# A one-core two-layer transformer kernel: eleven tile buffers, spaced row scatters and a later wait for counts in its tail

## What is computed

```
x = x + attn0(layernorm(x)) + ffn0(layernorm(x))
x = x + attn1(layernorm(x)) + moe(layernorm(x))
```

```
logits = xt @ Wg.T
topk_logits, topk_idx = top_k(logits, 2)
gates = zeros.at[rows, topk_idx].add(softmax(topk_logits))
h = gelu(einsum('th,ehi->tei', xt, W1) + b1)
y = einsum('te,teh->th', gates, einsum('tei,eih->teh', h, W2) + b2)
```

## Time and profile before

| what | value |
|---|---|
| median of 3 runs | 1271.79 us (1271.42 to 1272.31) |
| profiled execution, its own time | not listed |
| its span | 1269.4 us |
| mean granted TensorE clock | 0.982 |
| busy: PE, DVE, ACT, POOL | 1189.8, 848.0, 734.5, 665.2 us |
| chain that ended last | PE 63%, DVE 13%, ACT 10%, issue 6%, POOL 3%, DMA 3% |

### The profile page before, as it was taken

The page is one execution under the profiler, slowest core; times in us unless marked ns, Lnnn a source line. Parts: engine busy times, 40 slices in busy tenths (PEclk is TensorE's granted clock), DMA queues, the critical chain, the costliest instruction groups (busy, mean ns, idle before and its releaser), DMA issues.

```text
span 1269.4 us, 26751 instructions
## 1 busy us (share of the span) xinstructions
PE 1189.8 (94%) x9122; PEld 894.4 (70%) x9122; DVE 848.0 (67%) x3390; ACT 734.5 (58%) x1561; POOL 665.2 (52%) x921
## 2 busy tenths in 40 slices
PE   5988999999999999999999999999999857989996
PEld 2566777677767776777677767776776657885896
DVE  4066597659865986588658855886588646874563
ACT  2356367736773577357745774567456524557674
POOL 4574364536443644464446444644465436675677
PEclk9999999999999999999999999999999968999999
DMA  7704420432043304230423043304330056541333
GB/s 219 210 3 162 132 77 12 158 123 92 13 160 109 106 14 159 96 120 13 158 97 119 13 151 105 117 15 137 118 117 15 11 151 147 81 66 25 45 55 39
DMA packets 88039, 119.30 MB, mean 94 GB/s; under 512 B 13736, under 2 KB 46416, under 8 KB 85904
## 3 DMA queue, kind: packets, MB, share of 16 engines
q1 hardware_dynamic: 69312, 99.66, 25.2%
q0 software_dynamic: 13792, 9.54, 5.3%
q10 hardware_dynamic: 4800, 8.39, 2.0%
HBM read 70.78 MB, written 48.46 MB: 94 GB/s over the span
## 4 chain that ended last, share of the span: by engine, by line
PE 63%; DVE 13%; ACT 10%; issue 6%; POOL 3%; DMA 3%; SPq 0%; DVEq 0%; POOLq 0%; ACTq 0%
PE bank L708 18%; PE heads L766 13%; PE bank L701 12%; PE bank L680 7%; ACT probs L1119 5%; PE bank L676 3%; PE bank L691 2%; DVE xnT_s L1579 2%; POOL out L1361 2%; PE bank L1054 2%; DVE hrow L1579 2%; DVE hT_s L1579 2%; PE bank L816 2%; PE bank L1062 1%; PE bank L685 1%
## 5 line engine op out<-in xcount | busy, mean ns | idle before, releaser
L1119 ACT ACTIVATE probs<-bank 128x512 f32<-128x512 f32 (+2 forms) x896 | 443.3, 578 | 186.5 <-PE bank L708 180.2
L1308 POOL TENSOR_SCALAR_AFFINE_SELECT probs<-probs 128x384 f32<-128x384 f32 x256 | 127.4, 520 | 211.7 <-ACT probs L1119 211.2
L708 PE MATMUL bank<-K,Q 128*128 128x192 f32 (+4 forms) x1024 | 236.5, 308 | 0.0
L708 PE MATMUL bank<-Q,K 128*128 128x192 f32 (+4 forms) x1024 | 220.7, 322 | 3.3 <-ACT probs L1119 3.1
L766 PE MATMUL heads<-probs,V 128*18 128x192 f32 (+9 forms) x3072 | 196.1, 396 | 6.6 <-POOL probs L1311 3.9
L708 PEld LDWEIGHTS bank<-K,Q 128*128 128x128 f32 x1024 | 166.5, 189 | 21.7 <-issue 9.6
L708 PEld LDWEIGHTS bank<-Q,K 128*128 128x128 f32 x1024 | 152.3, 194 | 39.5 <-issue 17.5
L766 PEld LDWEIGHTS heads<-probs,V 128*9 128x9 f32 (+1 forms) x3072 | 78.5, 94 | 114.0 <-issue 75.6
L1361 POOL DMA_INDIRECT out<-h1T_s x78 | 123.1, 1578 | 60.0 <-ACT h1T_s L1269 35.6
L708 PE MATMUL bank<-QM,K 128*128 128x512 f32 (+3 forms) x512 | 138.4, 336 | 4.6 <-ACT probs L1119 3.8
L1261 ACT ACTIVATE h2T_s<-bank,h1T_s 128x128 f32<-128x128 f32 x312 | 89.2, 368 | 91.8 <-PE bank L1054 88.9
(11 more groups left out here) (224 smaller groups left out, 2184.9 us busy)
## 6 DMA issues: line engine op xcount, KB each, us to landing
Q<-slots_of_q SPq DMA_DIRECT2D x15, 1024.0 KB, 8.0
K<-low_of_h SPq DMA_DIRECT2D x13, 1024.0 KB, 7.8
QM<-slots_of_qm SPq DMA_DIRECT2D x8, 1024.0 KB, 6.0
K<-slots_of_k SPq DMA_DIRECT2D x60, 128.0 KB, 2.7
K<-slots_of_k SPq DMA_DIRECT2D x68, 96.0 KB
slots_of_q<-Q SPq DMA_DIRECT2D x24, 256.0 KB, 3.0
slots_of_k<-QM SPq DMA_DIRECT2D x24, 256.0 KB, 4.0
slots_of_qm<-Q SPq DMA_DIRECT2D x24, 256.0 KB, 4.2
```

The lines of the kernel that those rows point to most:

```text
L708: mm = pe.matmul(to[:, at:at + right.shape[1]], left, right, start=True, stop=True, skip_group_check=True)
L1119: return act.activation(to, bank, func, scale=scale, bias=bias).then_inc(taken_sem(run, unit), 1)
L1308: pool.affine_select(out=three, in_=three, compare_op=ALU.is_ge, fill=0.0, base=0, pattern=[[0, 3], [1, P]], channel_multiplier=-1)
```

## The change

- XB goes from 8 to 11. With it the early loads become tiles 0 to 10, then 11 and 12, the tail's loads start at tile 13, and run `lag` = 8 instead of 5 tiles ahead of `tiles_by(n)`, up to READY.
- `tile_xT` and `tile_b1` lie in w2T instead of behind the output buffers, since 11 * 130 + 4 * 128 leaves 106 values in `late`.
- SyncE waits for `pads_counted` behind the tail's first loads, ahead of the first pad, instead of ahead of everything in the tail.
- The eight scatters stand behind additions 16, 18, ... 30 instead of 16 to 23. The assertion holds with gated = 16.

```diff
-XB, OB, WB = 8, 4, 4
+XB, OB, WB = 11, 4, 4
...
-        tile_xT = late[:, XB * ROW + OB * P:XB * ROW + (OB + 2) * P].rearrange("p (n c) -> p n c", c=P)
-        tile_b1 = late[:, XB * ROW + (OB + 2) * P:XB * ROW + (OB + 2) * P + WB * FC].rearrange("p (n c) -> p n c", c=FC)
+        tile_xT = w2T[:, 0:2 * P].rearrange("p (n c) -> p n c", c=P)
+        tile_b1 = w2T[:, 2 * P:2 * P + WB * FC].rearrange("p (n c) -> p n c", c=FC)
...
                 run, lag = ("tail", NB), XB - 3
-                sp.wait_ge(S["pads_counted"], 1)
                 sp.wait_ge(S["routing_set"], ROUTING)
...
-                    if loaded < tiles_by(n) + lag:
-                        load_tiles(loaded, tiles_by(n) + lag)
-                        loaded = tiles_by(n) + lag
+                    if loaded < min(READY, tiles_by(n) + lag):
+                        load_tiles(loaded, min(READY, tiles_by(n) + lag))
+                        loaded = min(READY, tiles_by(n) + lag)
+                        if pads == 0:
+                            sp.wait_ge(S["pads_counted"], 1)
                         if pads < K2 * E:
...
             gated = tiles_by(9) + 1
+            assert gated + 2 * NT * K2 <= AT_MAXIMA + 1
             for i in range(QUERIED, AT_MAXIMA):
                 add_tile(i)
-                if gated <= i < gated + NT * K2:
-                    send_row((LAST, 0), i - gated)
+                if i in range(gated, gated + 2 * NT * K2, 2):
+                    send_row((LAST, 0), (i - gated) // 2)
```

## The result

| | before | after |
|---|---|---|
| median of 4 runs each | 1271.61 us (1269.51 to 1272.31) | 1262.49 us (1261.54 to 1266.1) |
| ratio, with its 95% interval | | 0.9931 (0.9914 to 0.9947) |
| profiled execution, its span | 1269.4 us | 1263.18 us, span 1261.4 us |
| mean granted TensorE clock | 0.982 | 0.983 |

The forecast was 1262.7 us. The medians stand 9.1 us apart, the ratio makes it 8.8 us, and the two spans 8.0. The last is smaller for a reason outside the change, shown at the end: in this execution the tail began 1.44 us later.

What follows compares the result with a forecast made beforehand. TensorE was taken to lose time at two places in the tail, before tile 10's load and from tile 28 on. Gains of 5.8 and 3.3 us, 9.1 together, gave 1262.7 us from 1271.79; 8-in-10 range 1260.7 to 1266.4.

Steps and rivals of the forecast that it cites:

- First stop: Tail start: tile 10 loaded early removes TensorE's 4.56 us wait and the low clock; tile 12 turned 5.8 us earlier.
- rival B: Tail start: the clock falls all the same after the pauses; 3.0 us lost, 1265.7 us; chance 0.09.
- Second stop: Tiles 27 to 32: spaced scatters keep GpSimd's backlog under the output buffers' limit, with 11 tile buffers; 3.3 us gained.
- Neither edit does this alone by my reckoning: Tiles 27 to 32: neither spaced scatters nor 11 tile buffers alone would bring the 3.1 to 3.6 us.
- The rest: Other effects of the edits, such as moved tiles, extra loads, counts' wait, pads and masks: nothing, or at most 0.5 lost.
- The three early loads: SyncE before the tail: they take 6.5 or 3.6 us of its 10.2 us wait for k2, so hidden.
- Rival D: Before the tail: extra loads block SyncE and the queries' fetch is late; 16 us lost, 1278.7 us; chance 0.03.
- Rival A: Scatter stretch: GpSimd stays the pace, its additions slowed by VectorE copies; 3.3 us not gained, 1266.0 us; chance 0.14.
- Rival C: More gain: VectorE's waits shrink by 1.0 us and the drain's 0.6 is had; 1261.1 us; chance 0.12.
- the drain's 0.6: Drain's end: GpSimd's 17 back-to-back additions might end 0.6 us earlier; counted as 0, at best 0.6.
- Sum: Whole kernel: 5.8 and 3.3 make 9.1 us gained; span 1260.3, time 1262.7 us.
- The 2.4 us that I kept between span and time: Whole kernel: the gap between profiled span 1269.4 and median 1271.79 us, assumed unchanged after the change.

Runs made afterwards that it cites:

- e10: The changed kernel run once more with nothing altered; 1262.04 us, ratio 0.9908 to the kernel before.
- e1: Kernel before with only the scatters spaced, behind additions 16, 18, ... 30; ratio 0.9973 to the kernel before.
- e5: Changed kernel with scatters back behind additions 16 to 23 and 8 output buffers instead of 4; ratio 0.9928 to the kernel before.
- e3: Kernel before with only 11 tile buffers and the transposed tiles in w2T; ratio 0.9953 to the kernel before.
- e6: Changed kernel with 8 tile buffers instead of 11; ratio 0.9936 to the kernel before.
- e4: Changed kernel with scatters put back behind additions 16 to 23; ratio 0.9949 to the kernel before.
- e9: As e8, with VectorE's choice of experts split in three parts between tiles; 1266.09 us, ratio 0.9943 to the kernel before.
- e8: Changed kernel with 8 output buffers and VectorE weighing the experts ahead of placing the rows; 1264.45 us, ratio 0.9927 to the kernel before.

## Why the prediction was right

**First stop: right, by its steps.** Moved to this profile's prefix product, 1.44 us later, the forecast for tiles 11 and 12 was 1071.7 and 1074.2 us; they came at 1071.70 and 1074.23. That it fits to a few hundredths is luck: in e10, the same kernel, tile 12 comes 0.42 us earlier behind the prefix product. The chain named for it is the one in the rows: ScalarE behind an addition (2.14 us), the second product of 8 behind ScalarE (1.24, forecast 1.5), VectorE's copy just in time. The clock held at its 2.4 GHz level behind that pause, and in every profile without the 4.5 us stop it was 1.00 from 1066 to 1142 us; where the stop is (before, and e1) it fell, to 0.52 over seven microseconds in both. So rival B did not happen here. How the 5.8 us divide into 2.8 for the stop and 3.0 for the clock no run took apart; the two always came and went together. And the low level is not tied to that stop alone, as the last section shows.

**Second stop: right in size and cause, wrong in one sentence.** 15.42 less 11.85 is 3.57 us; 3.1 to 3.6 was the working, 3.3 the term. e5 shows that the limit was the one the working used, four output buffers and GpSimd's backlog. The sentence that failed is "Neither edit does this alone by my reckoning". The spacing alone brings 2.95 (e1), the eleven buffers alone 1.30 (e3), and both 3.57. The half about the buffers was sound, OB's limit does hold with 11; but I took from it that spacing with eight buffers must also fall short, and never worked that out. The same working said that load 28 is late because addition 20 is, so a GpSimd that keeps its backlog small mends the loads as well, whatever the number of their buffers; that step was left out. Of the 0.6 us between 12.47 (e1) and 11.85, TensorE's waits tell: in e1 it stands 0.6 us, twice, for VectorE's copies between the transposes of tiles 27 and 32, and not at all in the kernel after; it is no wait for a load, and e6, with eight buffers too, has 12.00. One figure of the working is off by little: at the slowest landing 9.84 less 0.4 and 4.3 leaves 5.1 us of backlog, not 5.0.

**The rest: right.** The three early loads cost nothing. SyncE's timeline, kernel after, with the loads ahead of the tail:

```profile
1022.79 20.59 SPq L647 DMA_DIRECT2D h1T_s<-sorted_rows  x11
```

and its wait for ScalarE's part of k2:

```profile
SPq L494 <- ACT Q L1110: 6.7, 1, 6.7
```

SyncE's wait for k2 was 10.2 us before, so the three loads took 3.5 of it; 3.6 was the lower of the two prices. Rival D needed 10.1 us of delay and did not come near it. Rival A did not occur: GpSimd's timeline, kernel after, has one addition in the spaced stretch that took 2.08 us in place of 1.55, and its neighbours have the usual length or at most 0.15 more:

```profile
1096.45 2.08 POOL L1362 DMA_INDIRECT out<-h1T_s  x1 [0.30 <-issue]
```

Rival C had two halves. VectorE's waits did not shrink (2.0 us in the stretch, before and after), and of the drain's 0.6 GpSimd's last eighteen additions gave 0.4 (31.46 us from the first to the last against 31.84 in the earlier trace rows), but they began 0.4 later behind tile 38, so none of it is in the time.

**Sum.** 9.1 us were forecast, 5.8 and 3.3. In the profiles it is 9.26 up to tile 38, of which 5.83 and 3.57 lie in the two stops and 0.14 was lost beside them, and 9.21 to the last addition. The 2.4 us that I kept between span and time are not what one execution has, which is 1.8 in the profile after: 0.6 of them came from comparing the span of one execution with the median of several. Keeping them amounts to taking 9.1 from the median, so the sum is none the worse for it.

## What to carry to other kernels

When a list of waits names a load, ask what the load itself waited for, and go on to the last link: here the loads stood for additions, and mending the additions' pace ended the loads' waits in the second stop with the eight buffers there were. Where one slow queue gets bursts of extra work in the middle of a steady pace, spread them out so that the backlog stays under what the buffers behind it allow; a limit can be worked out beforehand as buffers times period, less processing and landing. And when single profiles of two kernels are compared, lay them over each other at an instruction both have just ahead of the change: the difference of their spans alone would have said that e4 is 3.4 us slower than e3.

## What the runs showed of the hardware

**A low clock early in the run goes with a later tail.** Windows of 120 to 130 us, code that all kernels share, kernel before and kernel after:

```profile
120.00:130.00 10.00, 8.70 (x69) 6.58 (x70) 7.23 (x10) 7.00 (x16) 7.21 (x8) 1.00 0.46 137
```

```profile
120.00:130.00 10.00, 8.88 (x35) 7.33 (x35) 8.28 (x11) 5.94 (x16) 8.22 (x8) 0.66 0.41 118
```

The counts of matmuls are no measure of speed here, since a group of 32 small ones starts at 127.57 us before and at 130.84 after, outside the window. One group of four matmuls, the same in both, in TensorE's timeline, again before and after:

```profile
123.55 1.16 PE L701 MATMUL bank<-probs_high,h1T_high 128*128 128x512 f32 x4 [0.46 <-DVE attn L1628]
```

```profile
124.77 2.04 PE L702 MATMUL bank<-probs_high,h1T_high 128*128 128x512 f32 x4
```

The kernel after is 1.22 us behind at these and 3.27 at 132 us, so this stretch costs some 2 us and the rest arose before it. SyncE's next load of `x_in`, a block of the input, is 3.05 us later (240.39 and 243.44). Over the twelve profiles the order is clean: three with a clock of 1.00 in that window have this load at 239.6 to 240.4 us, two with 0.83 at 241.3 and 241.8, seven with 0.66 to 0.68 at 242.9 to 244.0. Part of that is made up on the way, and between before and after the prefix product comes 1.44 later. What decides the clock there from one execution to the next was not found.

**The same pause lowers the clock in some executions and not in others.** TensorE stands some 3 us between 1054 and 1061 us in all of these kernels but e9. The mean clock from 1058 to 1066 is 1.00 in nine of the twelve profiles and 0.79 in three (e3, e4, e8); the rows of e3, and of the kernel after:

```profile
1058.00:1066.00 8.00, 8.00 (x60) 8.00 (x59) 4.39 (x14) 4.38 (x16) 6.80 (x6) 0.79 0.85 202
```

```profile
1058.00:1066.00 8.00, 6.53 (x58) 6.56 (x58) 6.67 (x20) 4.20 (x15) 7.11 (x5) 1.00 0.87 204
```

At 0.79 TensorE needs all 8.00 us for 60 matmuls; at 1.00 it does 58 in 6.53. From the product for the gates' logits to the prefix product the three take 15.35 to 15.39 us and the others, e9 apart, 13.68 to 13.91, so with the low clock the tail starts 1.5 us later. My argument that the clock holds after pauses of 3 and 1.5 us came out true in this kernel, but it rested on one execution.

**A copy on VectorE waits out a copy and a cast on GpSimd.** In e9 the 2.45 us of VectorE's weight copy (1063.37 to 1065.82), mostly 0.41 to 0.43, cover these rows of GpSimd's timeline, the second of them up to 0.04 us before its end:

```profile
1063.99 1.53 POOL L1339 COPY rows<-xn 128x1024 f32<-128x1024 f32 x1
1064.99 0.87 POOL L1340 CAST rows<-token 128x8 int32<-128x8 f32 x1
```

The same pair stands in all twelve profiles: in the kernel before VectorE's copy at 1061.07 us took 1.97 while GpSimd's ran from 1061.16, in the kernel after 1.98, and in the others 0.95 to 2.06, the shorter the later it starts. Each time it ends within 0.06 us of the end of GpSimd's cast. GpSimd's copy takes 1.5 to 1.6 us in all of them, so only VectorE is seen to pay. By the Trainium skill ("SBUF — State Buffer", Who interferes with whom) the two exclude each other on a shared pair of ports and the loser waits; these rows agree that one waits the other out. Why it is VectorE also where its row begins first (by 0.62 us in e9), they don't show. The additions that the rule made me fear for lost 0.5 us once in the spaced stretch, although VectorE copies weights for every tile.
